# Scaling Wh by a bound from x and W, and carrying the bound as column 129, in a graph network's opening stage

## The chip, the cores and the metric

The kernel runs on one core of a Trainium2 chip. The metric is the device time of one execution in microseconds (us); lower is better.

## The reference

Two graph layers over 8192 nodes with 128 features, each followed by a residual and a layer norm. The adjacency matrix is 8192 x 8192 in int32 and has ones on its diagonal and about 0.1% of the other places.

```python
Wh = h @ W
a1, a2 = (a[:Fout, 0], a[Fout:, 0])
e = (Wh @ a1)[:, None] + (Wh @ a2)[None, :]
e = jnp.where(e > 0, e, ALPHA * e)                    # ALPHA = 0.2
e = jnp.where(adj > 0, e, MASK_VAL)
attention = jax.nn.softmax(e, axis=1)
return jax.nn.elu(attention @ Wh)                     # layer 0
...
x1 = a @ x / deg                                      # layer 1
return jnp.concatenate([x1, x], axis=1) @ weight + bias
...
x = _layernorm(x + layer0(x, adj, W, a), axis=-1)
x = _layernorm(x + layer1(x, adj, weight, bias), axis=-1)
```

With s = Wh a1 and t = Wh a2, exp of a positive score is exp(s) exp(t), and of a negative one exp(0.2 s) exp(0.2 t). So the softmax's sums are matrix products of two 0/1 masks (score positive, score negative, each within the edges) with two scaled copies of Wh.

## The kernel before

**The pieces.** The nodes are cut into 64 blocks of 128 (j). Sixteen steps k of four blocks make Wh; 32 groups g of 256 rows make layer 0, each in eight eighths h of eight blocks; two eighths make a unit c. Five engines run their own lists in order and wait for each other by semaphores.

**x and Wh.** SyncE loads x in nine pieces. In step k TensorE transposes four tiles of x (`turn_x`), ScalarE copies them out and at the same time sums them over the nodes (`copy_turned`, L416), and TensorE multiplies them with W and its two products with a (`make_wh`, L617). VectorE copies s and t out of the result (L865), ScalarE copies Wh (`copy_wh`), and VectorE finds the largest absolute value of that piece (L871). W is transposed first of all, and W a (L597) made from it, before x is touched.

**The adjacency.** GpSimd issues transfers of chunks of 512 rows by 2048 columns, cast to bytes. TensorE packs a chunk to bits (`pack_bits`, L640), ScalarE copies the words (`copy_words`). VectorE unpacks them to edges (L936).

**The factors.** With t's maximum over all partitions (from GpSimd) ScalarE makes the columns exp(t - max) and exp(0.2 (t - max)). VectorE multiplies 16 blocks of Wh with one of them (`make_product`, L923: product n is unit n // 2, part n % 2), ScalarE scales and rounds to 16 bits (`high_of`, L504), and VectorE writes what is left as a second 16-bit half (`low_of`, L1028; `low_half`, L1037). The scale comes from the largest absolute value of Wh, which goes through GpSimd once more. Column 129 of each half holds the exponential itself, for the denominators; VectorE makes these columns by casts and subtractions of their own. x lies in the space of the second part of the factors until it is no longer needed.

**The masks.** ScalarE compares t of a block with s of 256 rows (a score, `first_scores` L436 for group 0, `scores` L466 later). VectorE ands the eight scores of an eighth with the edges (`negative`, L1013) and then xors the edges with that (`positive`, L1020). TensorE multiplies both masks with the factors (`multiply`, L679), 32 matmuls an eighth; within the first group an eighth also waits for the low halves of its unit. Later chunks are packed between the multiplications of a group.

**Order in the opening.** ScalarE turns s around for the store of s (L452), makes scores 0 to 9, words 0, high halves 0 and 1, words 1, scores 10 to 29, the columns for u and v, high halves 2 and 3, scores to 49, words 2, high halves 4 and 5, the other scores, words 3, eight scores of group 1, and high halves 6 and 7. VectorE makes for each unit both low halves, the four masks, and the next two products. The sum over x's nodes, needed for rows without edges, is a reduction of ScalarE's sums.

Of the kernel before, what the change touches and what calls it, by code (L numbers as in the profile page):

```python
# [50 lines left out]
WIDEST = 10.0  # L51
# [7 lines left out]
def adj_resnorm_kernel(nc, x, adj, w0, a0, w1, b1, consts, out):  # L59
# [21 lines left out]
    with ctx:  # L81
# [3 lines left out]
        def sem(name):  # L85
# [11 lines left out]
        cols = sb("cols", [P, 12, NJ], F32)  # L97
# [9 lines left out]
        wh_top = sb("wh_top", [P, NX], F32)  # L107
        x_sums = sb("x_sums", [P, NX], F32)
# [5 lines left out]
        s_col, t_col, t_big, e_col, f_col, u_col, v_col, y_col, uy_col, vy_col, e_den, f_den = \  # L114
            (cols[:, k, :] for k in range(12))
        t_max, _, wh_max, wh_one, neg_t, neg_ft, inv_wh, scale_e, ones, sum_x = (one[:, k:k + 1] for k in range(10))
# [10 lines left out]
        wh = words[:, NG // 2:, :].rearrange("p g w -> p (g w)").bitcast(F32)[:, 0:NJ * F]\  # L127
            .rearrange("p (j f) -> p j f", f=F)
        early = words[:, 2:NG // 2, :].rearrange("p g w -> p (g w)").bitcast(F32)
        sizes, at, early_of = dict(product=3 * UNIT * F, wq=F + 2, w_turn=P, a_sb=2,  # L130
# [4 lines left out]
        product = early_of["product"].rearrange("p (k j f) -> p k j f", k=3, f=F)  # L135
        x_in = factors[:, 1, :, :].rearrange("p j r -> p (j r)").bitcast(F32)[:, 0:NJ * F]\
            .rearrange("p (k j f) -> p k j f", k=NX, f=F)
        x_t = product[:, 2, 0:2 * XB, :].rearrange("p (k j) f -> p k (j f)", k=2)
# [213 lines left out]
        def _(pool):  # L352
# [49 lines left out]
        def _(act):  # L402
# [3 lines left out]
            act.wait_ge(w0_turned, 1)  # L406
            act.activation(w_turn, turn_ps[0][:, 0:P], ACT.Copy).then_inc(w_turn_ok, 1)
            act.wait_ge(wa_made, 1)
            act.activation(wq[:, F:F + 2], turn_ps[1][:, 0:2], ACT.Copy).then_inc(wa_ok, 1)
# [15 lines left out]
            def copy_wh(k):  # L425

                act.wait_ge(wh_ok, k + 1)
                act.activation(wh[:, XB * k:XB * (k + 1), :].rearrange("p (h j) f -> p h j f", h=2),
                               wh_banks(k)[:, :, :, 0:F], ACT.Copy).then_inc(wh_copied, 1)
# [23 lines left out]
            first_scores(0, 2)  # L453


# [3 lines left out]
            first_scores(2, 10)  # L459
# [40 lines left out]
            def high_of(n):  # L500
# [3 lines left out]
                act.activation(factors[:, n % 2, (n // 2) * UNIT:(n // 2 + 1) * UNIT, 0:F], product[:, n % 3, :, :],  # L504
                               ACT.Copy, scale=scale_e).then_inc(high_ok, 1)
# [83 lines left out]
        def _(pe):  # L589
# [3 lines left out]
            pe.wait_ge(w0_in, 16)  # L593
            pe.transpose(turn_ps[0][:, 0:P], wq[:, 0:F], ident).then_inc(w0_turned, 1)
            pe.wait_ge(w_turn_ok, 1)
            pe.wait_ge(a0_in, 16)
            pe.matmul(turn_ps[1][:, 0:2], w_turn, a_sb, start=True, stop=True).then_inc(wa_made, 1)  # L597
            pe.wait_ge(wa_ok, 1)
            pe.wait_ge(ones_ok, 1)

# [10 lines left out]
            def make_wh(k):  # L611

                pe.wait_ge(x_t_ok, k + 1)
                if k >= 2:
                    pe.wait_ge(wh_copied, k - 1)
# [28 lines left out]
            def spread_s():  # L644

                pe.wait_ge(wh_ok, 1)
                for j in range(2 * TPG):
                    m = pe.matmul(pack_ps[1][:, j * P:(j + 1) * P], s_col[:, j:j + 1].to_broadcast([P, P]), ident,
                                  start=True, stop=True)
                m.then_inc(s_spread, 1)  # L650

            turn_x(0)
            for k in range(NX):
                if k + 1 < NX:
                    turn_x(k + 1)
# [42 lines left out]
            pe.wait_ge(wh_copied, NX)  # L698
            pack_bits(1)
            wide = is_wide(pe)  # L700
            pe.wait_ge(sum_xb_ok, 1)
            pe.matmul(turn_ps[1][:, 0:F], sum_xb, wq[:, 0:F], start=True, stop=True).then_inc(mean_made, 1)
            pe.wait_ge(den_hi_ok, 4)
            pe.wait_ge(edge_col_ok, 1)
            for c in range(UPG):
                for h in (2 * c, 2 * c + 1):
                    multiply(0, h, c == UPG - 1 or h % 2 == 0, True)
                if c < 2:
                    pack_bits(c + 2)
            group(1, {1: (1, 0), 2: (1, 1), 3: (1, 2)})  # L710
# [134 lines left out]
        def _(dve):  # L845
# [16 lines left out]
            def copy_s_t(k):  # L862

                dve.wait_ge(wh_made, k + 1)
                dve.tensor_copy(cols[:, 0:2, XB * k:XB * (k + 1)].rearrange("p k (h j) -> p h j k", h=2),  # L865
                                wh_banks(k)[:, :, :, F:F + 2]).then_inc(wh_ok, 1)

            def largest_wh(k):

                dve.wait_ge(wh_copied, k + 1)  # L870
                dve.tensor_reduce(wh_top[:, k:k + 1], wh[:, XB * k:XB * (k + 1), :], AX.XY,  # L871
                                  ALU.max, apply_absolute_value=True).then_inc(top_ok, 1)

            def scaled_t(c):

                dve.wait_ge(wh_ok, XB * (c + 1))
# [478 lines left out]
```

## Time and profile before

| | |
|---|---|
| time, median of 3 runs | 1486.75 us (1486.2 to 1486.85) |
| span of the profiled execution | 1484.3 us |
| what lies around the span, against the median | 2.45 us |
| TensorE busy | 1449.9 us (98%) |
| VectorE busy | 994.9 us (67%) |
| ScalarE busy | 936.4 us (63%) |
| GpSimd busy | 118.3 us (8%) |
| mean granted TensorE clock | 0.991 |

The span is from the first to the last instruction of the profiled execution; its own time beyond the span isn't recorded, so the median stands for it. Busy shares are averages over stages with different limits; a line such as L679 is a line of the kernel. PE is TensorE's matmul, PEld its weight load, DVE VectorE, ACT ScalarE, POOL GpSimd. The granted clock is 1.00 at 2.4 GHz and 0.50 at 1.2 GHz.

### The profile page before, as it was taken

The page shows a single profiled execution, that of the slowest core. Times are in us where ns is not written, and L with a number is a line of the kernel's source. Part 1 is how long each engine was busy: PE and PEld are TensorE (multiplying, and loading weights), DVE is VectorE, ACT ScalarE, POOL GpSimd, SP SyncE. Part 2 cuts the span into 40 slices and gives each one's busy share as a digit, 9 for nine tenths or more (in the row PEclk, how much of TensorE's full clock was granted, in tenths as well). Part 3 has the DMA queues.
Part 4 walks back from the last instruction along what each step waited for, and adds up shares of the span by engine and source line. Part 5 has one row for each costly group of instructions (what it writes and reads, how often), then busy time and mean ns, then how long its engine had stood idle before and what let it go on. Part 6 is the DMA issues. An engine that isn't in the chain of part 4 may idle for free.

```text
span 1484.3 us, 33988 instructions
## 1 busy us (share of the span) xinstructions
PE 1449.9 (98%) x12110; PEld 1107.8 (75%) x12110; DVE 994.9 (67%) x2833; ACT 936.4 (63%) x2289; POOL 118.3 (8%) x199
## 2 busy tenths in 40 slices
PE   7599999999999999999999999999999999999998
PEld 7578888888888888888888888884454545454557
DVE  4998888888788888878887887773433343334332
ACT  6989999999999999999999999940000000000000
POOL 1001000100010010001000100000000000000000
PEclk9799999999999999999999999999999999999999
DMA  9969997788788868877886882041000000000000
GB/s 174 111 71 101 120 108 90 83 94 95 84 86 96 93 78 95 94 90 82 95 94 83 87 96 37 19 119 49 22 15 21 14 21 14 21 14 21 14 15 15
DMA packets 99201, 101.47 MB, mean 68 GB/s; under 512 B 4432, under 2 KB 66384, under 8 KB 99152
## 3 DMA queue, kind: packets, MB, share of 16 engines
q0 software_dynamic: 33792, 67.11, 45.5%
q1 hardware_dynamic: 64800, 33.57, 8.7%
q8 instruction: 31, 0.51, 0.1%
q10 hardware_dynamic: 560, 0.14, 0.1%
q14 instruction: 18, 0.15, 0.0%
HBM read 289.48 MB, written 12.65 MB: 204 GB/s over the span
## 4 chain that ended last, share of the span: by engine, by line
PE 90%; DMA 2%; DVE 1%; issue 0%; POOL 0%; ACT 0%; SPq 0%; DVEq 0%; POOLq 0%
PE acc L679 58%; PE pack_ps L758 27%; PE pack_ps L819 2%; DMA adj_space<-in_adj 2%; PE acc L793 1%; PE pack_ps L628 1%; PE turn_ps L780 1%; PE turn_ps L769 0%; DMA level_ring<-x_rows 0%; DMA x_parts<-parts 0%; POOL one L378 0%; DVE adj_space L945 0%; DVE stats L1118 0%; DVE part_sums L1051 0%; DVE edge_ring L1020 0%
## 5 line engine op out<-in xcount | busy, mean ns | idle before, releaser
L466 ACT ACTIVATE level_ring<-s_row,cols 128x256 fp8e4<-128x256 f32 x1984 | 803.7, 495 | 0.0
L679 PE MATMUL acc<-factors,edge_ring 128*128 128x259 f16 x4096 | 548.8, 274 | 14.5 <-DVE edge_ring L1020 13.0
L679 PE MATMUL acc<-factors,level_ring 128*128 128x259 f16 x4096 | 548.3, 274 | 0.0
L758 PE MATMUL pack_ps<-adj_space,factors 128*128 128x512 fp8e4 x1920 | 421.7, 379 | 0.9 <-issue 0.9
L679 PEld LDWEIGHTS acc<-factors,edge_ring 128*128 128x128 fp8e4 x4096 | 365.9, 98 | 64.8 <-issue 15.8
L679 PEld LDWEIGHTS acc<-factors,level_ring 128*128 128x128 fp8e4 x4096 | 366.5, 98 | 48.9
L758 PEld LDWEIGHTS pack_ps<-adj_space,factors 128*128 128x128 f16 x1920 | 187.9, 98 | 217.6 <-issue 1.1
L1013 DVE TENSOR_TENSOR level_ring<-level_ring,edge_ring 128x1024 uint16<-128x1024 uint16 x256 | 171.2, 689 | 103.7 <-ACT level_ring L466 93.3
L1190 DVE TENSOR_SCALAR adj_space<-words 128x512 uint16 (+1 forms) x448 | 96.3, 288 | 146.7 <-PE pack_ps L758 146.6
L628 PE MATMUL pack_ps<-pack_w,adj_space 128*128 128x32 bf16 x960 | 170.7, 178 | 0.0
L1020 DVE TENSOR_TENSOR edge_ring<-edge_ring,level_ring 128x1024 uint16<-128x1024 uint16 x256 | 166.7, 683 | 0.1
L558 ACT ACTIVATE level_ring<-turn_ps 128x512 f32<-128x512 f32 x16 | 9.6, 597 | 217.4 <-PE turn_ps L769 217.4
L566 ACT ACTIVATE level_ring<-pack_ps 128x256 f32<-128x256 f32 x30 | 9.9, 381 | 212.6 <-PE pack_ps L758 212.6
L936 DVE TENSOR_SCALAR edge_ring<-words 128x512 uint16 (+1 forms) x448 | 106.1, 297 | 8.6 <-issue 6.4
L376 POOL TENSOR_SCALAR one<-mv 128x2 f32<-128x2 f32 x64 | 18.9, 295 | 1075.1 <-DVE mv L1125 1075.1
L628 PEld LDWEIGHTS pack_ps<-pack_w,adj_space 128*128 128x128 fp8e4 x960 | 91.6, 95 | 14.1
L1219 DVE SCALAR_TENSOR_TENSOR level_ring<-acc,cols,level_ring 128x128 f32<-128x128 f32 x64 | 19.4, 346 | 96.8 <-PE acc L793 96.8
L945 DVE SCALAR_TENSOR_TENSOR adj_space<-adj_space 128x1024 int32<-128x1024 int32 x60 | 73.1, 1218 | 0.9 <-DMA adj_space<-in_adj 0.9
L358 POOL DMA_DIRECT2D adj_space<-in_adj x64 | 51.3, 802 | 260.5 <-PE pack_ps L628 195.8
L422 ACT ACTIVATE words<-pack_ps 128x512 f32 (+1 forms) x64 | 38.1, 595 | 39.7 <-PE pack_ps L628 39.7
L378 POOL TENSOR_TENSOR one<-one 128x2 f32<-128x2 f32 x64 | 48.0, 750 | 9.5
L1130 DVE TENSOR_SCALAR level_ring<-level_ring,mv,one 128x128 f32<-128x128 f32 x64 | 19.3, 344 | 41.5 <-POOL one L378 41.5
(104 smaller groups left out, 726.8 us busy)
## 6 DMA issues: line engine op xcount, KB each, us to landing
adj_space<-in_adj POOLq DMA_DIRECT2D x64, 1024.0 KB, 14.5
rows_x<-in_x SPq DMA_DIRECT2D x32, 128.0 KB, 2.1
x_rows<-rows_y SPq DMA_DIRECT2D x32, 128.0 KB, 9.7
x_parts<-parts SPq DMA_DIRECT2D x32, 128.0 KB, 4.4
factors<-x_parts SPq DMA_DIRECT2D x8, 512.0 KB, 4.8
level_ring<-x_rows SPq DMA_DIRECT2D x16, 256.0 KB, 2.8
out<-level_ring SPq DMA_DIRECT2D x32, 128.0 KB, 1.8
s_row<-s_and_t SPq DMA_DIRECT2D x30, 128.0 KB, 3.0
```

The lines of the kernel that those rows point to most:

```text
L358: pool.dma_start(adj_ring[:, c, :, :], adj_tiles[n, :, :, c * COLS:(c + 1) * COLS]).then_inc(adj_in[c], 16)
L378: pool.tensor_tensor(rstd, var_eps, minus_half, ALU.pow).then_inc(rstd_sem, TPG)
L422: act.activation(row_words[:, n, c * WPU:(c + 1) * WPU], pack_ps[c % 2][:, 0:WPU], ACT.Copy)\
L466: a = act.activation(level_bytes[:, h % MASK_SLOTS, j, :], s_row[:, slot, :], ACT.Relu, bias=t_big[:, h * HALF + j:h * HALF + j + 1], scal ...
L628: return pe.matmul(pack_ps[c % 2][:, j * WPR:(j + 1) * WPR], nibbles, pack_w[:, 0, :], start=True, stop=True)
L679: m = pe.matmul(acc[a][:, 0:WIDE_ROW], mask, factors[:, neg, jj, 0:WIDE_ROW], start=(jj == 0), stop=(jj == NJ - 1))
L758: m = pe.matmul(pack_ps[slot][:, :], factors[:, 0, jj, part * F:(part + 1) * F], ring_1_bytes[:, c, j, :], start=(jj == 0 and part == 0), ...
L936: d = dve.tensor_scalar(to, src, 6 - k, EDGES, ALU.logical_shift_left, ALU.bitwise_and)
L945: dve.scalar_tensor_tensor(out=pair[:, 0], in0=pair[:, 1], scalar=1, in1=pair[:, 0], op0=ALU.logical_shift_left, op1=ALU.bitwise_or).then_ ...
L1013: dve.tensor_tensor(level, level, edge_ring[:, c % EDGE_SLOTS, k * HALF:(k + 1) * HALF, :], ALU.bitwise_and).then_inc(neg_ready, 1)
L1020: dve.tensor_tensor(edges, edges, level_ring[:, (2 * c + k) % MASK_SLOTS, :, :], ALU.bitwise_xor)\
L1190: d = dve.tensor_scalar(to, src, 6 - k, EDGES, ALU.logical_shift_left, ALU.bitwise_and)
```

## The change

All of it lies in the opening, up to the end of group 0.

- The scale of the factors no longer comes from the largest value of Wh, but from a bound: the largest absolute value of x, found on VectorE as x's pieces land (`top_of_x`), times the largest sum of absolute values over W. GpSimd makes both maxima in one call, before Wh is complete.
- Wh, s and t lie together, 130 columns a block. Even steps are copied by ScalarE (`copy_wh`), odd ones by VectorE (`keep_wh`), all 130 columns at once. Once s has been copied to its own columns, its place in each block gets the bound. VectorE's products are then 129 columns wide, and so are the high and low halves: the denominators' columns come with them, and their casts and subtractions go.
- The sum of x over the nodes is made by TensorE with a column of ones (`sum_rows_of_x`), behind the first pack, ahead of the transposition of s. x's space is needed until then, so high half 1 and a memset wait for it. VectorE copies and spreads the sum (`sum_of_x`).
- The columns y, uy and vy are made by GpSimd.
- W is transposed after x's first tile.
- The orders of ScalarE and VectorE in group 0 are written anew.
- The limit of t's spread from which another, slower path is taken goes from 10 to 7.5.

```diff
-WIDEST = 10.0
+WIDEST = 7.5
...
-        cols = sb("cols", [P, 12, NJ], F32)
+        cols = sb("cols", [P, 10, NJ], F32)
...
+        early = words[:, 2:, :].rearrange("p g w -> p (g w)").bitcast(F32)
+        sizes, at, early_of = dict(wh=NJ * (F + 2), product=3 * UNIT * FD, wq=F + 2, w_turn=P, a_sb=2,
...
+        wh_s_t = early_of["wh"].rearrange("p (j f) -> p j f", f=F + 2)
+        wh, wh_top = wh_s_t[:, :, 0:F], wh_s_t[:, :, 0:FD]
+        s_of, t_of = wh_s_t[:, :, F], wh_s_t[:, :, F + 1]
...
@@ gpsimd
+            pool.wait_ge(x_top_ok, NX // 2 + 2)
+            pool.wait_ge(w_sums_ok, 1)
+            pool.partition_all_reduce(tops[:, 2:4], tops[:, 0:2], P, bass.bass_isa.ReduceOp.max).then_inc(x_w_ok, 1)
             pool.wait_ge(t_top_ok, 1)
             pool.wait_ge(low_ok, 2)
             pool.partition_all_reduce(top_low[:, 2:4], top_low[:, 0:2], P, bass.bass_isa.ReduceOp.max).then_inc(t_max_ok, 1)
-            pool.wait_ge(wh_one_ok, 1)
-            pool.partition_all_reduce(wh_max, wh_one, P, bass.bass_isa.ReduceOp.max).then_inc(wh_max_ok, 1)
+            pool.wait_ge(t_max_ok, 1)
+            pool.wait_ge(cols_ok, 1)
+            pool.tensor_tensor(y_col, s_col, t_max.to_broadcast([P, NJ]), ALU.add).then_inc(y_ok_col, 1)
...
@@ scalar
-                act.activation(x_t[:, k % 2, :], turn_ps[k % 2][:, :], ACT.Copy, accum_out=x_sums[:, k:k + 1])\
-                    .then_inc(x_t_ok, 1)
+                act.activation(x_t[:, k % 2, :], turn_ps[k % 2][:, :], ACT.Copy).then_inc(x_t_ok, 1)
...
-            for k in range(NX):
+            copy_turned(0)
+            act.wait_ge(w0_turned, 1)
+            act.activation(w_turn, pack_ps[0][:, 0:P], ACT.Copy).then_inc(w_turn_ok, 1)
+            copy_turned(1)
+            act.wait_ge(wa_made, 1)
+            act.activation(wq[:, F:F + 2], pack_ps[0][:, P:P + 2], ACT.Copy).then_inc(wa_ok, 1)
+            copy_wh(0)
+            for k in range(2, NX):
                 copy_turned(k)
...
-                if k:
+                if k % 2:
                     copy_wh(k - 1)
-            copy_wh(NX - 1)
-            act.wait_ge(s_row_ok, 1)
-            act.wait_ge(s_turned, 1)
-            act.activation(s_turn, turn_ps[0][:, 0:P], ACT.Copy).then_inc(s_turn_ok, 1)
-            first_scores(0, 2)
+                if k >= 6:
+                    first_scores(k - 6, k - 5)
+            first_scores(10, 12)
+            copy_words(0, 0)
+            act.wait_ge(cols_ok, 1)
             act.wait_ge(neg_ok, 2)
             act.activation(e_col, t_col, ACT.Exp, bias=neg_t).then_inc(exp_cols_ok, 1)
             act.activation(f_col, t_col, ACT.Exp, bias=neg_ft, scale=ALPHA).then_inc(exp_cols_ok, 1)
-            first_scores(2, 10)
+            first_scores(12, 16)
+            act.wait_ge(s_turned, 1)
+            act.activation(s_turn, turn_ps[0][:, 0:P], ACT.Copy).then_inc(s_turn_ok, 1)
...
-            copy_words(0, 0)
             high_of(0)
+            first_scores(16, 20)
+            act.wait_ge(sum_made, 1)
             high_of(1)
+            first_scores(20, 24)
             copy_words(0, 1)
-            first_scores(10, 30)
+            first_scores(24, 32)
+            high_of(2)
+            high_of(3)
+            first_scores(32, 40)
+            copy_words(0, 2)
+            high_of(4)
+            high_of(5)
+            first_scores(40, 56)
+            high_of(6)
+            copy_words(0, 3)
+            first_scores(56, 64)
+            high_of(7)
             act.wait_ge(uy_ok, 2)
...
-            high_of(2)
-            high_of(3)
-            first_scores(30, 50)
-            copy_words(0, 2)
-            high_of(4)
-            high_of(5)
-            first_scores(50, 64)
-            copy_words(0, 3)
             scores(1, 1, 0)
-            high_of(6)
-            high_of(7)
...
@@ tensor
+            def sum_rows_of_x():
+
+                pe.wait_ge(ones_ok, 1)
+                for k in range(NX):
+                    for j in range(XB):
+                        m = pe.matmul(turn_ps[1][:, 0:1], x_in[:, k, j, :], ones, start=(k + j == 0),
+                                      stop=(k == NX - 1 and j == XB - 1))
+                m.then_inc(sum_made, 1)
...
-            pe.wait_ge(wh_ok, NX)
-            pe.transpose(turn_ps[0][:, 0:P], cols[:, 0:2, :].rearrange("p k j -> p (k j)"), ident).then_inc(s_turned, 1)
             pe.wait_ge(pack_w_ok, 2 * TILES - 1)
             pack_bits(0)
+            sum_rows_of_x()
+            pe.wait_ge(cols_ok, 1)
+            pe.transpose(turn_ps[0][:, 0:P], cols[:, 0:2, :].rearrange("p k j -> p (k j)"), ident).then_inc(s_turned, 1)
...
                     if factors_in and a < 2:
+                        pe.wait_ge(edge_col_ok, neg + 1)
                         pe.wait_ge((e_low_ok, f_low_ok)[neg], min(h // 2, UPG - 1) + h // 7 + 1)
...
@@ vector
+            def top_of_x(k):
+
+                dve.wait_ge(x_in_sem[k], 16)
+                first, end = max(2 * k - 1, 0), min(2 * k + 1, NX)
+                dve.tensor_reduce(x_top[:, k:k + 1], x_in[:, first:end], AX.XYZ, ALU.max, apply_absolute_value=True)\
+                    .then_inc(x_top_ok, 1)
+
+            def keep_wh(k):
 
                 dve.wait_ge(wh_made, k + 1)
-                dve.tensor_copy(cols[:, 0:2, XB * k:XB * (k + 1)].rearrange("p k (h j) -> p h j k", h=2),
-                                wh_banks(k)[:, :, :, F:F + 2]).then_inc(wh_ok, 1)
-
-            def largest_wh(k):
...
+                dve.tensor_copy(wh_s_t[:, XB * k:XB * (k + 1), :].rearrange("p (h j) f -> p h j f", h=2), wh_banks(k))\
+                    .then_inc(wh_kept, 1)
...
+            dve.tensor_scalar(wh_one, x_most, w_most, 1e-30, ALU.mult, ALU.max).then_inc(wh_one_ok, 1)
...
-            make_product(0)
-            scale_of_wh()
-            make_product(1)
-            for col, den in ((e_col, e_den), (f_col, f_den)):
-                dve.tensor_scalar(den, col, E_SCALE, None, ALU.mult).then_inc(den_ok, 1)
...
-            for c in range(UPG - 1):
-                low_of(2 * c, e_low_ok)
-                low_of(2 * c + 1, f_low_ok)
-                masks(0, 0, c)
-                make_product(2 * c + 2)
-                make_product(2 * c + 3)
-            last_masks_of_first()
...
+            def sum_of_x():
+
+                dve.wait_ge(sum_made, 1)
+                dve.tensor_copy(sum_x, turn_ps[1][:, 0:1]).then_inc(sum_x_ok, 1)
+                dve.wait_ge(sum_x_ok, 1)
+                dve.tensor_scalar(sum_xb, ident, 0.0, sum_x, ALU.mult, ALU.add).then_inc(sum_xb_ok, 1)
+
+            first_unpack(0)
+            make_product(0)
+            split(0, 0)
+            make_product(1)
+            low_of(0, e_low_ok)
+            split(0, 1)
+            dve.wait_ge(sum_made, 1)
+            dve.memset(factors[:, 1, :, ROW:WIDE_ROW], 1.0).then_inc(edge_col_ok, 1)
+            low_of(1, f_low_ok)
+            make_product(2)
+            first_unpack(1)
+            make_product(3)
+            split(1, 0)
+            split(1, 1)
+            low_of(2, e_low_ok)
+            low_of(3, f_low_ok)
+            make_product(4)
+            make_product(5)
+            first_unpack(2)
+            split(2, 0)
+            split(2, 1)
+            low_of(4, e_low_ok)
+            low_of(5, f_low_ok)
+            make_product(6)
+            make_product(7)
+            sum_of_x()
...
+            for k in range(2):
+                low_half(2 * UPG - 2, k, e_low_ok)
+                if k == 0:
+                    unpack(0, 0, UPG - 1, edge_ring, UPG - 1).then_inc(unpacked, 1)
+                low_half(2 * UPG - 1, k, f_low_ok)
+                negative(0, UPG - 1, k)
+                positive(0, UPG - 1, k)
```

## Rows read from the trace of the kernel before

**Rows 1.** Busy time by stretch; columns: engines' busy us (instructions), TensorE clock, DMA share, GB/s.
```profile
0.00:93.20 93.20, 67.38 (x718) 59.45 (x719) 70.71 (x130) 79.42 (x169) 7.38 (x15) 0.87 1.06 137
93.20:920.00 826.80, 825.91 (x8168) 728.43 (x8169) 677.10 (x1735) 775.28 (x1921) 77.08 (x112) 1.00 0.79 89
```

**Rows 2.** Waits of TensorE, first 200 us: us in total, times, longest.
```profile
PE acc L679 <- DVE edge_ring L1020: 13.0, 4, 7.3
```

**Rows 3.** Timeline of the opening: start, us, engine, line, operation, idle before.
```profile
7.14 0.56 PE L597 MATMUL turn_ps<-words 128*128 128x2 f32 x2 [1.62 <-DMA words<-in_a]
...
9.85 2.10 PE L617 MATMUL acc<-words 128*128 128x130 f32 x8
...
12.55 1.06 PE L617 MATMUL acc<-words 128*128 128x130 f32 x8
...
30.76 2.36 PE L617 MATMUL acc<-words 128*128 128x130 f32 x16
...
33.55 1.75 PE L640 MATMUL pack_ps<-pack_w,adj_space 128*128 128x32 bf16 x64
...
35.64 2.29 DVE L923 TENSOR_TENSOR words<-words,cols 128x2048 f32<-128x2048 f32 x1
...
39.35 3.89 ACT L504 ACTIVATE factors<-words,one 128x2048 f16<-128x2048 f32 x2
...
42.05 0.50 PEld L702 LDWEIGHTS turn_ps<-words 128*128 128x128 f32 x2 [1.06 <-DVE words L965]
...
50.12 1.89 PE L679 MATMUL acc<-factors,edge_ring 128*128 128x259 f16 x8 [7.28 <-DVE edge_ring L1020]
...
80.48 1.29 DVE L1037 SCALAR_TENSOR_TENSOR factors<-words,one,factors 128x1024 f16<-128x1024 f32 x1 [0.60 <-ACT factors L504]
...
88.12 0.69 DVE L1020 TENSOR_TENSOR edge_ring<-edge_ring,level_ring 128x1024 uint16<-128x1024 uint16 x1
...
93.21 1.05 PE L679 MATMUL acc<-factors,edge_ring 128*128 128x259 f16 x8 [0.54 <-DVE part_sums L1051]
```

**Rows 4.** Groups by form, first 93 us: busy us, mean ns, idle before.
```profile
L436 ACT ACTIVATE level_ring<-s_row,cols 128x256 fp8e4<-128x256 f32 x64 | 26.0, 497 | 0.0
...
L923 DVE TENSOR_TENSOR words<-words,cols 128x2048 f32<-128x2048 f32 x8 | 18.0, 2285 | 0.1
...
L504 ACT ACTIVATE factors<-words,one 128x2048 f16<-128x2048 f32 x8 | 15.7, 1995 | 0.9 <-DVE words L923 0.9
...
L1028 DVE SCALAR_TENSOR_TENSOR factors<-words,one,factors 128x2048 f16<-128x2048 f32 x6 | 14.0, 2373 | 0.2 <-ACT factors L504 0.2
...
L640 PE MATMUL pack_ps<-pack_w,adj_space 128*128 128x32 bf16 x256 | 7.1, 179 | 3.9 <-issue 3.9
...
L1013 DVE TENSOR_TENSOR level_ring<-level_ring,edge_ring 128x1024 uint16<-128x1024 uint16 x10 | 6.5, 687 | 0.1
...
L1037 DVE SCALAR_TENSOR_TENSOR factors<-words,one,factors 128x1024 f16<-128x1024 f32 x4 | 5.1, 1284 | 0.6 <-ACT factors L504 0.6
...
L936 DVE TENSOR_SCALAR edge_ring<-words 128x512 uint16<-128x512 uint16 x19 | 4.5, 297 | 0.1
...
L422 ACT ACTIVATE words<-pack_ps 128x512 uint16<-128x512 f32 x4 | 2.3, 578 | 0.0
...
L597 PE MATMUL turn_ps<-words 128*128 128x2 f32 x2 | 0.6, 348 | 1.6 <-DMA words<-in_a 1.6
```

**Rows 5.** Busy time and granted clock around the falls and rises.
```profile
33.50:36.40 2.90, 1.80 (x65) 1.69 (x65) 2.77 (x12) 2.63 (x8) 1.26 (x3) 1.00 1.05 107
36.40:50.10 13.70, 2.67 (x66) 2.30 (x67) 13.44 (x27) 13.70 (x28) 1.17 (x2) 0.50 1.06 116
50.10:53.20 3.10, 3.08 (x15) 2.16 (x16) 3.10 (x3) 2.38 (x7) 0.00 (x0) 0.50 1.07 107
71.20:74.00 2.80, 0.00 (x0) 0.00 (x0) 2.77 (x7) 2.80 (x8) 0.74 (x1) 0.99 1.06 108
74.00:80.10 6.10, 5.08 (x24) 3.57 (x25) 5.88 (x5) 6.10 (x12) 0.00 (x0) 0.50 1.05 116
```

More of the change, by code:

```diff
@@ L113, in adj_resnorm_kernel @@
         ident = consts_sb[:, 0:P]
-        s_col, t_col, t_big, e_col, f_col, u_col, v_col, y_col, uy_col, vy_col, e_den, f_den = \
-            (cols[:, k, :] for k in range(12))
-        t_max, _, wh_max, wh_one, neg_t, neg_ft, inv_wh, scale_e, ones, sum_x = (one[:, k:k + 1] for k in range(10))
+        s_col, t_col, t_big, e_col, f_col, u_col, v_col, y_col, uy_col, vy_col = \
+            (cols[:, k, :] for k in range(10))
+        x_most, w_most, _, wh_one, neg_t, neg_ft, inv_wh, scale_e, ones, sum_x = (one[:, k:k + 1] for k in range(10))
+        x_most, w_most = tops[:, 2:3], tops[:, 3:4]
         t_max, t_spread = top_low[:, 2:3], wide_one[:, 7:8]
@@ L592, in _ @@
             pe.wait_ge(consts_in, 16)
[L593 to L599, printed above, removed]
             def turn_x(k):
@@ L709, in _ @@
                     pack_bits(c + 2)
+                if c == 2:
+                    pe.wait_ge(sum_xb_ok, 1)
+                    pe.matmul(turn_ps[1][:, 0:F], sum_xb, wq[:, 0:F], start=True, stop=True).then_inc(mean_made, 1)
             group(1, {1: (1, 0), 2: (1, 1), 3: (1, 2)})
@@ L880, in _ @@
-            for k in range(NX):
-                copy_s_t(k)
-                if 0 < k < NX - 1:
-                    largest_wh(k - 1)
-                if k % XB == XB - 1 and k < NX - 1:
-                    scaled_t(k // XB)
-            dve.wait_ge(wh_ok, NX)
-            dve.tensor_reduce(top_low[:, 1:2], t_col, AX.X, ALU.min).then_inc(low_ok, 1)
-            dve.tensor_reduce(top_low[:, 0:1], t_col, AX.X, ALU.max).then_inc(t_top_ok, 1)
+                dve.tensor_scalar(t_big[:, js], t_of[:, js], -BIG, None, ALU.mult).then_inc(t_big_ok, 1)
@@ new lines, in _ @@
+            top_of_x(0)
+            dve.wait_ge(w_turn_ok, 1)
+            dve.tensor_reduce(tops[:, 1:2], w_turn, AX.X, ALU.add, apply_absolute_value=True).then_inc(w_sums_ok, 1)
+            top_of_x(1)
+            top_of_x(2)
+            keep_wh(1)
+            top_of_x(3)
+            top_of_x(4)
+            keep_wh(3)
+            scaled_t(0)
+            top_of_x(5)
+            keep_wh(5)
+            top_of_x(6)
+            keep_wh(7)
+            scaled_t(1)
+            top_of_x(7)
@@ new lines, in _ @@
+            top_of_x(8)
+            dve.wait_ge(x_top_ok, NX // 2 + 1)
+            dve.tensor_reduce(tops[:, 0:1], x_top[:, :], AX.X, ALU.max).then_inc(x_top_ok, 1)
+            keep_wh(9)
+            keep_wh(11)
+            scaled_t(2)
+            dve.wait_ge(x_w_ok, 1)
+            dve.tensor_scalar(wh_one, x_most, w_most, 1e-30, ALU.mult, ALU.max).then_inc(wh_one_ok, 1)
+            dve.wait_ge(wh_one_ok, 1)
+            dve.reciprocal(inv_wh, wh_one).then_inc(inv_ok, 1)
+            dve.wait_ge(inv_ok, 1)
@@ L902, in _ @@
             dve.tensor_scalar(wide_flag[:, :], t_spread, WIDEST, None, ALU.is_gt).then_inc(wide_ok, 1)
-            def scale_of_wh():
-                dve.wait_ge(wh_max_ok, 1)
-                dve.tensor_scalar(wh_one, wh_max, 1e-30, None, ALU.max).then_inc(guard_ok, 1)
-                dve.wait_ge(guard_ok, 1)
-                dve.reciprocal(inv_wh, wh_one).then_inc(inv_ok, 1)
-                dve.wait_ge(inv_ok, 1)
-                dve.tensor_scalar(scale_e, inv_wh, E_SCALE, None, ALU.mult).then_inc(scale_ok, 1)
+            dve.memset(factors[:, 0, :, ROW:WIDE_ROW], 1.0).then_inc(edge_col_ok, 1)
             def make_product(n):
@@ L1027, in low_of @@
                 dve.wait_ge(high_ok, n + 1)
-                dve.scalar_tensor_tensor(out=factors[:, k, js, FD:FD + F], in0=product[:, n % 3, :, :], scalar=scale_e,
-                                         in1=factors[:, k, js, 0:F], op0=ALU.mult, op1=ALU.subtract)\
+                dve.scalar_tensor_tensor(out=factors[:, k, js, FD:ROW], in0=product_of[n], scalar=scale_e,
+                                         in1=factors[:, k, js, 0:FD], op0=ALU.mult, op1=ALU.subtract)\
                     .then_inc(done, 1)
@@ L1036, in low_half @@
                 dve.wait_ge(high_ok, n + 1)
-                dve.scalar_tensor_tensor(out=factors[:, part, js, FD:FD + F],
-                                         in0=product[:, n % 3, k * HALF:(k + 1) * HALF, :], scalar=scale_e,
-                                         in1=factors[:, part, js, 0:F], op0=ALU.mult, op1=ALU.subtract).then_inc(done, 1)
+                dve.scalar_tensor_tensor(out=factors[:, part, js, FD:ROW],
+                                         in0=product_of[n][:, k * HALF:(k + 1) * HALF, :], scalar=scale_e,
+                                         in1=factors[:, part, js, 0:FD], op0=ALU.mult, op1=ALU.subtract).then_inc(done, 1)
             def add_negative(g, first=False):
```

122 lines of the change are left out of this document (53 added, 69 removed).

## Prediction

> **What bounds the kernel now.** I read the busy time of the engines by stretch first. In the first 93.2 us TensorE is busy for 67.38 us; from 93.2 to 920 us it is busy for all but a microsecond [rows 1]. So whatever the change does to the moment at which group 1's first multiplication starts (93.21 us) is carried to the end one for one: no later stage has idle time of TensorE in which a delay could vanish or to which a gain could be lost. The change touches nothing behind that moment.
>
> The waits of TensorE say who sets it: its longest, 13.0 us in four pieces, are for the masks that VectorE writes (L1020) [rows 2]. In the timeline the 16 products of x and W end at 33.1 us, VectorE's first product starts at 35.64, ScalarE's first high half at 39.35, group 0's first multiplication at 50.12, VectorE's last mask of group 0 starts at 88.12 and is done at 88.8; TensorE then has one eighth of the group left and starts group 1 at 93.21 [rows 3]. Between 36.4 and 80 us VectorE is busy in nearly all of the stretches shown that have work for TensorE or wait for it (13.44 of 13.70, 3.10 of 3.10, 5.88 of 6.10) [rows 5]. So the opening is VectorE's list of work: 8 products, 8 low halves, 4 unpacks, 8 mask pairs. I call its end E; before, E = 88.8.
>
> **What the change does to VectorE's list.** Prices by form [rows 4]: a product 2.285 (2.25 in a row, 18.0 over 8), a low half of 16 blocks 2.37 (2.31 in a row), a half of it 1.28, an unpack of four 0.9 (19 took 4.5), a mask pair (and, then xor, 0.69 each with a little overlap) 1.33, and on ScalarE a high half 1.96 (15.7 over 8), a copy of words 0.58, one score 0.405 (26.0 over 64). The 129th column makes a product 2064 elements instead of 2048, under 1% of 2.285, 0.02 each, 0.3 over all sixteen. Gone from the list are the denominators' casts and subtractions, y, uy, vy and the scale chain, some 2.5 us between the first product and the first low half; new are the copy and spreading of the sum, 0.65, and a memset, 0.17. The nine reductions of x, the copies of odd blocks and the scale found from the bound run while TensorE works through x (16 steps of 12 matmuls, 0.11 us apart: 1.06 less the last one's 0.287, over 7; 1.33 us a step). A step pair asks of VectorE about 1.2 + 0.65 and of ScalarE about 2.3 of 2.66 us (estimates from the spacing of their copies and scores), so TensorE stays the slower, and the stage's cost stays hidden; it would show if they passed 2.66. W's transposition moves behind x's first tile, which lets Wh begin about 1 us earlier. The end of x's stage then is about 32.1 instead of 33.1, and the first chunk is packed by 33.9 (1.75 us) [rows 3]. The maximum of t still has to go round through GpSimd, and an unpack now stands ahead of the first product, so that ends at about 38.5, against 37.9 before.
>
> List without waits: 4 unpacks 3.6, 8 products 18.2, 6 low halves 13.9, 4 halves of one 5.1, 8 mask pairs 10.6, the new 0.8: 52.2 us from 35.2, hence E = 87.4. That is the most that the list itself can give, 1.4 us. Three waits stand in it.
>
> **The sum of x on TensorE.** Before, x's sum fell out of ScalarE's copies. Now TensorE makes it, by 64 products of an f32 tile of x with one column, and it comes right behind the first pack. An f32 product that is no transposition is two instructions in this trace (L597: 128x2, x2), so 128 weight loads. The spacing of one: L597's two starts are 0.21 us apart (0.56 less 0.348), in a stretch in which L617's matmuls too ran at half of their later speed (2.10 for eight at 9.85, 1.06 at 12.55); the two loads of L702, at granted clock 0.50, take 0.50 us together, which fits a spacing near 0.2 and a last load that outlasts it [rows 3 to 5]. At full clock the nearest f32 rows are L617's, 0.11 apart with 130 columns: the upper bound. The lower bound is the pack's fp8 loads, 0.025 apart (1.75 less 0.18, over 63). I take the f32 rows with few columns, 0.20 at half clock and 0.105 at full.
>
> The Trainium skill ("TensorE: Matmul & The Clock Gate", sections "LDWEIGHTS (loading the stationary operand)" and "Weight-path perf modes — Fast Weight Load (FWL) and DoubleRow") has 107 ns for a load of 128 columns and the fast load for all but FP32; by it the sum would take 13.7 us at full clock, against 3.2 by the fp8 rows, and it speaks against the low end.
>
> Which clock? The nearest rows: the clock stood at 1.00 while the pack ran and at 0.50 one microsecond behind its end, at 36.4; the next pack and the two products behind it (2.67 us busy) ran at 0.50 and did not bring it back; the first multiplications of group 0 still had 0.50 for 3.1 us before it rose [rows 5]. After an idle stretch from 71.2 it fell at 74.0, 2.9 us in. I take it that the sum, one column each, lets it fall to 1.2 GHz some 2 us in: 20 loads at 0.105 and 108 at 0.20, S = 2.1 + 21.6 = 23.7 us. Full clock throughout: 128 x 0.105 = 13.4.
>
> What is queued behind it: on TensorE the transposition of s (0.5 us at half clock), then the pack of chunk 1; on ScalarE, whose order has the wait for that transposition *ahead of the first high half*, everything; on VectorE the low halves. High half 0 starts at T = 33.9 + S + 0.5 + 0.3 (the copy of s), so 58.4 with S = 23.7, against 39.35 before. VectorE has by then done two products, an unpack and one mask pair (42.0) and stands idle until T + 1.96. The chunk-1 pack, held to 39.2 by its transfer before, now ends near T + 1.5; ScalarE copies its words at T + 7.1, before VectorE asks for them at T + 10.4, so that costs nothing more.
>
> **Two waits in the new order.** (a) VectorE's mask pair (2,1) needs the scores up to 47. ScalarE makes them behind high half 5, which waits for product 5: 1.96 + 8 x 0.405 = 5.2 us after that product, where VectorE is ready after an unpack and one pair, 2.2. Idle: 3.0. (b) Low half 7 needs high half 7, which ScalarE makes after high half 6, a copy of words and 8 scores: 1.96 + 0.58 + 3.24 + 1.96 = 7.7 after product 6, while VectorE gets there after product 7, the sum's copy, a half and an unpack: 2.25 + 0.65 + 1.28 + 0.9 = 5.1. Idle: 2.6. Before, the same places lost 0.6 together [rows 3], since the scores to 49 were made before high half 4, and high half 7 followed 6 directly.
>
> **The sum.** From T on VectorE has 1.96 (waiting), 2.35, 1.33, 0.17, 2.35, 2.27, 0.9, 2.27, 2.66, 4.62, 4.49, 0.9, 2.66, 4.62, 4.49, 0.65, 1.28, 0.9, 1.28, 1.33, 2.5, 1.33 = 47.3, and 5.6 of the two waits: E = T + 52.9 = 111.3, 22.5 later than before. At the end TensorE has waited over 6 us for mask pair 6 (from the end of eighth 5 at T + 43 to T + 49), so that it starts eighth 6 at 0.50, as it did at 75 us after a shorter gap; that took 5 to 6 us where full clock takes 3.6 [rows 5], and about 1 us of it is left when group 1 begins. Together +23.5. The profiled execution's span is 1484.3 and the median 1486.75, so 2.45 us lie around the span and stay: **1510**, own range 1503 to 1515 (clock falling 1 to 3 us in, loads of 0.18 to 0.21).
>
> **Rivals.** *The clock holds* (S = 13.4): TensorE has no gap in the sum, and so far only gaps stood ahead of each fall. T = 48.1, E = 101.0, +12.2, and the 1 us: 1500 (1497 to 1503). For it: the clock fell only behind the pack's end. Against: narrow work at 36 to 50 us did not raise it. The skill's page on TensorE, section "HAM oscillation — how this bites in real kernels", puts the loss down to idle gaps alone; by that rule the clock would hold here, and the time would be this rival's.
>
> *The sum is cheap*, with loads as fast as the fp8 ones or nearly: up to S = 5.3 ScalarE has high half 0 ready when VectorE wants it at 42.0, and only the waits (a) and (b) are left: E = 87.4 + 5.6 = 93.0, +4.2, +1: 1492 (1490 to 1495). Against it: no f32 load in the trace is closer than 0.1 us.
>
> *Faster*: Wh's early start is worth more than I put it. Before, the first step of Wh starts at 9.85 and the second at 12.55, two steps' time at half speed; if TensorE is at full speed by then, and a0's landing at 7.1 is all that holds it, x's stage ends up to 3 us earlier, and with the shorter list E would be 84.4, 1482. It decides only if the sum's end stays under 39 and ScalarE stays ahead at (a) and (b); each of these alone outweighs it. About as unlikely is no change, from parts of both.
>
> That the constant WIDEST goes from 10 to 7.5 changes nothing: t's spread, estimated from the reference's factors (0.06, 0.06, 128 features), is about 3.6.
>
> **Chances.** Clock falls 0.52, clock holds 0.28, cheap sum 0.10, no change 0.05, faster 0.05. A measurement here tells 0.2% (3 us) from no change, so slower 0.90. The range: 1494 to 1515 holds nearly all of the first two and a corner of the third, 0.8.
>
> **What would show it.** The sum's 128 instructions behind the first pack, their spacing and the granted clock; ScalarE idle before the copy of s and VectorE idle before the first low half until T + 2; idle of 3.0 before the mask pair (2,1) (for ScalarE's scores) and 2.6 before low half 7; VectorE's last mask of group 0 at 111; all distances after group 1's start as before. The prediction is wrong if f32 loads with one column come much faster than 0.1 us, if x's stage grows, or if any wait of TensorE behind 93 us shrinks.

## The result, and the profile after

The changed kernel takes 1510.0 us (median of 5 runs, 1509.23 to 1510.21), against 1486.75 us for the kernel before (median of 5, 1486.2 to 1488.15): a ratio of 1.0153, with a 95% interval of 1.014 to 1.0165. It is 23.25 us slower. The span of its profiled execution is 1507.3 us, 23.0 more than before.

Busy time by stretch of the kernel after, in the columns of [rows 1]. The first two lines are the rest from group 1's start, cut at the same distance as before; the others follow the sum of x.

```profile
117.65:944.45 826.80, 826.80 (x8179) 729.35 (x8177) 677.68 (x1735) 779.50 (x1930) 75.61 (x112) 1.00 0.79 89
944.45:1507.30 562.85, 555.60 (x3217) 318.98 (x3215) 245.88 (x967) 80.60 (x199) 33.82 (x72) 1.00 0.09 26
...
34.60:36.00 1.40, 1.40 (x19) 1.40 (x15) 1.25 (x10) 1.22 (x4) 0.35 (x1) 1.00 1.04 113
36.00:37.00 1.00, 1.00 (x11) 1.00 (x10) 1.00 (x5) 1.00 (x3) 0.00 (x0) 1.00 1.09 109
37.00:38.00 1.00, 1.00 (x10) 1.00 (x9) 1.00 (x1) 0.56 (x2) 0.00 (x0) 0.89 1.04 104
38.00:39.00 1.00, 1.00 (x7) 1.00 (x6) 1.00 (x2) 0.00 (x0) 0.00 (x0) 0.50 1.05 106
39.00:58.80 19.80, 19.80 (x95) 19.80 (x95) 3.33 (x3) 0.00 (x0) 2.05 (x4) 0.50 1.06 108
```

From 34.6 to 58.8 us TensorE is busy without a gap, and all the same the granted clock goes from 1.00 to 0.50 within the two microseconds from 37. Ahead of the fall the products start 0.11 us apart (the first at 34.59, the 29th at 37.71), behind it 0.213 (the 30th at 37.88, the 128th and last at 58.79). In the last stretch shown VectorE is busy for 3.33 of 19.80 us and ScalarE not at all: both wait.

The timeline of the opening of the kernel after, as in [rows 3].

```profile
8.83 2.10 PE L623 MATMUL acc<-words 128*128 128x130 f32 x8 [0.53 <-ACT words L449]
11.58 1.94 PE L623 MATMUL acc<-words 128*128 128x130 f32 x8
14.03 1.06 PE L623 MATMUL acc<-words 128*128 128x130 f32 x8
...
32.98 1.75 PE L646 MATMUL pack_ps<-pack_w,adj_space 128*128 128x32 bf16 x64
...
34.59 24.55 PE L663 MATMUL turn_ps<-one,factors 128*128 128x1 f32 x128
...
46.30 0.48 POOL L377 TENSOR_SCALAR cols<-cols 128x64 f32<-128x64 f32 x1
...
59.49 0.28 ACT L470 ACTIVATE words<-turn_ps 128x128 f32<-128x128 f32 x1 [21.93 <-PE turn_ps L685]
59.67 2.02 ACT L515 ACTIVATE factors<-words,one 128x2064 f16<-128x2064 f32 x1
61.73 2.37 DVE L1033 SCALAR_TENSOR_TENSOR factors<-words,one,factors 128x2064 f16<-128x2064 f32 x1 [19.36 <-ACT factors L515]
65.41 2.44 DVE L1033 SCALAR_TENSOR_TENSOR factors<-words,one,factors 128x2064 f16<-128x2064 f32 x1
...
90.09 0.69 DVE L1018 TENSOR_TENSOR level_ring<-level_ring,edge_ring 128x1024 uint16<-128x1024 uint16 x1 [3.09 <-ACT level_ring L439]
...
105.97 1.29 DVE L1042 SCALAR_TENSOR_TENSOR factors<-words,one,factors 128x1032 f16<-128x1032 f32 x1 [2.94 <-ACT factors L515]
...
108.89 1.39 PE L703 MATMUL acc<-factors,edge_ring 128*128 128x259 f16 x8 [4.64 <-DVE edge_ring L1025]
111.64 0.69 DVE L1025 TENSOR_TENSOR edge_ring<-edge_ring,level_ring 128x1024 uint16<-128x1024 uint16 x1
117.65 1.05 PE L703 MATMUL acc<-factors,edge_ring 128*128 128x259 f16 x8
...
174.18 1.23 DVE L984 SCALAR_TENSOR_TENSOR adj_space<-adj_space 128x1024 int32<-128x1024 int32 x1 [0.47 <-DMA adj_space<-in_adj]
```

Read the brackets in order. The 128 instructions of the sum take 24.55 us. ScalarE, whose copy of s stands behind them, waits 21.93 us for it, and so the first high half starts at 59.67 instead of 39.35. VectorE waits 19.36 us for that half, then 3.09 us ahead of the mask pair (2,1) for scores, and 2.94 us for high half 7. Its last mask ends at E = 111.64 + 0.69 = 112.33 us; before it was 88.12 + 0.69 = 88.81. So E is 23.5 us later, which is the size of the loss.

### The profile page after: what moved, and what is told of

Read it like the earlier page. It is cut to its first block, busy times and chain, and to the rows that moved or that the text cites. A ratio compares the mean times of both kernels' runs of the same rounds, so it can differ in the third digit from the quotient of the medians.

```text
span 1507.3 us, 34219 instructions
## 1 busy us (share of the span) xinstructions
PE 1476.8 (98%) x12238; PEld 1134.1 (75%) x12238; DVE 998.4 (66%) x2813; ACT 931.4 (62%) x2265; POOL 117.9 (8%) x202
## 4 chain that ended last, share of the span: by engine, by line
PE 95%; DVE 2%; ACT 1%; DMA 1%; issue 1%; POOL 0%; SPq 0%; DVEq 0%; POOLq 0%
PE acc L703 60%; PE pack_ps L780 27%; PE pack_ps L841 2%; PE turn_ps L663 2%; PE acc L623 1%; PE pack_ps L634 1%; PE acc L815 1%; PE turn_ps L802 1%; DVE words L962 1%; ACT level_ring L439 1%; PE turn_ps L614 1%; DVE factors L1033 1%; PE turn_ps L791 0%; ACT factors L515 0%; DMA factors<-in_x 0%
## 5 line engine op out<-in xcount | busy, mean ns | idle before, releaser
L1270 DVE SCALAR_TENSOR_TENSOR level_ring<-acc,cols,level_ring 128x128 f32<-128x128 f32 x64 | 19.4, 346 | 96.7 <-PE acc L815 96.7
```

## The experiments

Two theories stand against each other. By the first, three things add up: the sum's length, which is long because its one-column products run at the low clock, and the waits (a) and (b), which come from ScalarE's order alone. By the rival, the loss lies in what the change needs anyway, wider products, new waits or x's stage, and the sum is only where it shows. Each time stands beside the kernel before, run on the same chip.

**The sum with 128 columns.** The same 128 weight loads, but each multiplies 128 columns of ones instead of one.

```diff
-                        m = pe.matmul(turn_ps[1][:, 0:1], x_in[:, k, j, :], ones, ...
+                        m = pe.matmul(turn_ps[1][:, 0:P], x_in[:, k, j, :], ones.to_broadcast([P, P]), ...
```

> The sum's 128 matmuls stream 128 columns of ones instead of one; the loads are the same. If the fall of the clock sets their spacing (my theory), wide matmuls behind the pack keep full clock, the spacing goes to 0.11 us, the sum takes 14 us instead of 24.5 and the kernel 1499 to 1501 us. If a load of f32 weights is 0.2 us apart for another reason than the clock, the time stays at 1509 to 1511 or grows, with the sum at 24 us or more. If the sum isn't what delays the opening, no change either, but with a sum of 14 us.

Measured: 1498.63 us beside 1487.21, ratio 1.0076 [1.006, 1.0093]. Its timeline, and then its clock during the sum:

```profile
34.16 14.54 PE L663 MATMUL turn_ps<-one,factors 128*128 128x128 f32 x128
...
101.00 0.69 DVE L1025 TENSOR_TENSOR edge_ring<-edge_ring,level_ring 128x1024 uint16<-128x1024 uint16 x1
```

```profile
34.20:48.50 14.30, 14.30 (x133) 14.30 (x130) 7.56 (x16) 2.78 (x7) 2.10 (x5) 1.00 1.06 108
```

128 times the columns, and the sum is 10.0 us shorter. The clock stands at 1.00 throughout, and the spacing is (14.54 - 0.27)/127 = 0.112 us, the 0.11 of the f32 rows with 130 columns. One-column products have it too, ahead of the fall. E comes 10.6 us earlier, the span is 10.5 us shorter (1496.8), and the loss against the kernel before goes from 23.25 to 11.4 us. So 10 of the 24.55 us are the clock's; the other 14.5 are the 128 loads with their products at the high level.

**The sum back on ScalarE.** x's sum falls out of ScalarE's copies again, and no engine waits for a sum of TensorE any more; nothing else is undone.

```diff
-                act.activation(x_t[:, k % 2, :], turn_ps[k % 2][:, :], ACT.Copy).then_inc(x_t_ok, 1)
+                act.activation(x_t[:, k % 2, :], turn_ps[k % 2][:, :], ACT.Copy, accum_out=x_sums[:, k:k + 1])\
+                    .then_inc(x_t_ok, 1)
...
-            act.wait_ge(sum_made, 1)
...
-            sum_rows_of_x()
...
-                dve.wait_ge(sum_made, 1)
-                dve.tensor_copy(sum_x, turn_ps[1][:, 0:1]).then_inc(sum_x_ok, 1)
+                dve.wait_ge(x_t_ok, NX)
+                dve.tensor_reduce(sum_x, x_sums[:, :], AX.X, ALU.add).then_inc(sum_x_ok, 1)
```

> The sum over x's nodes goes back to ScalarE's copies, as in the kernel before; nothing waits for TensorE's sum any more, all else as changed. My theory: ScalarE starts high half 0 near 38.8 us, VectorE's list runs on from 42.4, its last mask is done near 93.3 instead of 112.3, and the time is 1490 to 1492. Rival, the 129 columns and the new list are what costs: over 1500. Rival, the copies with a sum slow x's stage by more than 1 us: 1493 or more.

Measured: 1491.06 us beside 1487.21, ratio 1.0026 [1.0016, 1.0036]: 19.4 of the 23.25 us are gone. Its timeline:

```profile
41.60 2.36 DVE L1033 SCALAR_TENSOR_TENSOR factors<-words,one,factors 128x2064 f16<-128x2064 f32 x1
...
70.07 0.69 DVE L1018 TENSOR_TENSOR level_ring<-level_ring,edge_ring 128x1024 uint16<-128x1024 uint16 x1 [3.09 <-ACT level_ring L441]
...
85.96 1.29 DVE L1042 SCALAR_TENSOR_TENSOR factors<-words,one,factors 128x1032 f16<-128x1032 f32 x1 [2.96 <-ACT factors L517]
...
91.62 0.69 DVE L1025 TENSOR_TENSOR edge_ring<-edge_ring,level_ring 128x1024 uint16<-128x1024 uint16 x1
```

The first low half is back at 41.60, without a wait. Both waits are still there, (a) with 3.09 us and (b) with 2.96: they belong to the order, not to the sum. E is 92.31. The copies with a sum do not slow x's stage: the pack starts at 32.30 here, at 32.98 in the kernel after.

**s turned ahead of the sum.** The transposition of s moves from behind the sum to ahead of it, so that ScalarE and high half 0 no longer wait.

```diff
             pack_bits(0)
-            sum_rows_of_x()
             pe.wait_ge(cols_ok, 1)
             pe.transpose(turn_ps[0][:, 0:P], cols[:, 0:2, :].rearrange("p k j -> p (k j)"), ident).then_inc(s_turned, 1)
+            sum_rows_of_x()
```

> The transposition of s stands ahead of the sum on TensorE, so that ScalarE's first high half no longer waits for the sum; high half 1 and VectorE's memset still do. My theory: VectorE goes on from low half 1 at 61.6 us instead of 65.4, so 3 to 4 us are won: 1506 to 1507. Rival, the wait ahead of high half 0 is the whole loss: 1490 to 1492.

Measured: 1506.55 us beside 1487.21, ratio 1.0129 [1.0112, 1.0145]. Its timeline:

```profile
35.36 24.93 PE L663 MATMUL turn_ps<-one,factors 128*128 128x1 f32 x128
...
60.33 2.04 ACT L515 ACTIVATE factors<-words,one 128x2064 f16<-128x2064 f32 x1 [17.40 <-PE turn_ps L663]
62.40 2.37 DVE L1033 SCALAR_TENSOR_TENSOR factors<-words,one,factors 128x2064 f16<-128x2064 f32 x1 [1.69 <-ACT factors L515]
...
108.56 0.69 DVE L1025 TENSOR_TENSOR edge_ring<-edge_ring,level_ring 128x1024 uint16<-128x1024 uint16 x1
```

Only 3 to 4 us come back (E by 3.1). The wait moves one place down: high half 1 writes where x lies, so it must wait for the sum in any order, 17.40 us here. The order of the two on TensorE is a small part; that x's space is held is the larger one.

**ScalarE's order.** The sum stays; the scores that a mask pair needs are made before the next high halves, and words 3 and the last scores before high half 6.

```diff
-            first_scores(32, 40)
+            first_scores(32, 48)
             copy_words(0, 2)
             high_of(4)
             high_of(5)
-            first_scores(40, 56)
-            high_of(6)
+            first_scores(48, 64)
             copy_words(0, 3)
-            first_scores(56, 64)
+            high_of(6)
             high_of(7)
```

> Only ScalarE's order in group 0 changes: scores 32 to 47 ahead of high half 4, scores 48 to 63 and words 3 ahead of high half 6, so that high half 7 follows 6 directly. My theory: the waits of 3.1 us (scores) and 2.9 us (high half 7) go, and 0.6 comes back: 1504 to 1505. Rival, they are hidden by TensorE's own work at the end of group 0: 1509 to 1510.

Measured: 1503.09 us beside 1487.21, ratio 1.0107 [1.009, 1.0124]: 7 us come back, a little more than the 6.03 us of both waits. Its timeline:

```profile
94.86 2.03 ACT L515 ACTIVATE factors<-words,one 128x2064 f16<-128x2064 f32 x1 [1.48 <-DVE words L961]
...
97.08 2.03 ACT L515 ACTIVATE factors<-words,one 128x2064 f16<-128x2064 f32 x1 [0.18 <-DVE words L961]
...
105.03 0.69 DVE L1024 TENSOR_TENSOR edge_ring<-edge_ring,level_ring 128x1024 uint16<-128x1024 uint16 x1
...
110.12 1.05 PE L702 MATMUL acc<-factors,edge_ring 128*128 128x259 f16 x8 [0.39 <-DVE part_sums L1055]
...
170.49 1.05 PE L702 MATMUL acc<-factors,edge_ring 128*128 128x259 f16 x8 [1.06 <-DVE part_sums L1055]
```

Now it is ScalarE that waits for VectorE's products at the last two high halves. E is 105.72, 6.6 us earlier, and group 1 starts 4.40 us after it, as before (4.40), instead of 5.32. The last line shown, a wait of TensorE in a later stage, is taken up with the prediction's last term below.

**Both.** The edits of the second and the fourth experiment together.

> Both repairs together: the sum on ScalarE's copies and ScalarE's order without the two waits. If the two losses add (my theory), VectorE's list runs without a wait of more than 0.6 us, its last mask is done near 86 to 88 us and the time is 1484 to 1486, so the rest of the change is worth 0 to 3 us. Rival, the 129 columns and VectorE's copies in x's stage cost as much as the denominators did: 1487 or more.

Measured: 1484.51 us beside 1487.37, ratio 0.998 [0.9971, 0.9989]: 2.9 us faster than the kernel before, and the fastest here. Its timeline:

```profile
8.52 2.10 PE L623 MATMUL acc<-words 128*128 128x130 f32 x8 [0.62 <-ACT words L451]
11.26 1.29 PE L623 MATMUL acc<-words 128*128 128x130 f32 x8
...
32.22 1.75 PE L646 MATMUL pack_ps<-pack_w,adj_space 128*128 128x32 bf16 x64
...
45.21 2.44 DVE L1032 SCALAR_TENSOR_TENSOR factors<-words,one,factors 128x2064 f16<-128x2064 f32 x1
45.46 2.49 POOL L378 TENSOR_SCALAR cols<-cols 128x64 f32<-128x64 f32 x1
...
85.22 0.69 DVE L1024 TENSOR_TENSOR edge_ring<-edge_ring,level_ring 128x1024 uint16<-128x1024 uint16 x1
90.31 1.05 PE L702 MATMUL acc<-factors,edge_ring 128*128 128x259 f16 x8 [0.39 <-DVE part_sums L1055]
```

E is 85.91, 2.9 us ahead of 88.81, and group 1 starts 2.9 us earlier. Alone the two edits gained 19.4 and 7.4 us, 26.8 in sum; together they gained 26.1 (23.25 + 2.86). So the sum and ScalarE's order make up all of the loss, and the rest of the change taken together (the bound, the 129th column with its wider products, VectorE's copies and order, the place of W) is a gain of 2.9 us.

**Three products on GpSimd.** On top of that, products 3, 5 and 7 are made by GpSimd, which is nearly idle, in the place of Wh. GpSimd then issues some of group 1's transfers of adjacency between them.

```diff
+            def pool_product(n):
...
+                pool.tensor_tensor(product_of[n], wh_top[:, js, :],
+                                   f_col[:, js].unsqueeze(2).to_broadcast([P, UNIT, FD]), ALU.mult)\
+                    .then_inc(pool_product_ok, 1)
...
-            make_product(3)
+            make_product(4)
...
-            make_product(4)
-            make_product(5)
+            make_product(6)
...
-            make_product(6)
-            make_product(7)
```

> As the run with both repairs, and GpSimd makes products 3, 5 and 7, in place in Wh, while VectorE goes on with masks. If VectorE's list is the bound of the opening, 3 x 2.27 = 6.8 us go from it, of which ScalarE's own list (scores, high halves, words: 39 us from 35.9 on) lets at most 5 through: 1480 to 1482. Rival, a product on GpSimd takes over 8 us or slows VectorE, so that the high halves wait for it: 1486 or more.

Measured: 1489.7 us beside 1487.37, ratio 1.0018 [1.0009, 1.0027], 5.2 us slower than without. Its timeline, POOL against DVE:

```profile
53.17 8.29 POOL L402 TENSOR_TENSOR words<-words,cols 128x2064 f32<-128x2064 f32 x2
...
53.84 4.12 DVE L1037 TENSOR_TENSOR level_ring<-level_ring,edge_ring 128x1024 uint16<-128x1024 uint16 x1
57.99 4.01 DVE L1044 TENSOR_TENSOR edge_ring<-edge_ring,level_ring 128x1024 uint16<-128x1024 uint16 x1
61.93 0.68 DVE L1037 TENSOR_TENSOR level_ring<-level_ring,edge_ring 128x1024 uint16<-128x1024 uint16 x1
...
70.20 4.21 POOL L402 TENSOR_TENSOR words<-words,cols 128x2064 f32<-128x2064 f32 x1 [7.99 <-DVE words L981]
70.95 4.01 DVE L1037 TENSOR_TENSOR level_ring<-level_ring,edge_ring 128x1024 uint16<-128x1024 uint16 x1
```

A GpSimd product takes some 4.2 us, and the VectorE mask that starts during it takes 4.0 to 4.1 us instead of 0.69; the first mask behind it takes 0.68 again. Three masks lose 10 us, and three products of 2.3 us save 7: 3 us of the loss. The other 2 us were not taken apart by a run. In this trace the pack starts 0.8 us later than in "both" (33.03), and group 1 starts 6.44 us after VectorE's last mask (96.69 against 90.25) instead of 4.40. The Trainium skill ("SBUF — State Buffer", section "Who interferes with whom") says that VectorE and GpSimd share a pair of ports as an exclusive lock, and that an instruction of VectorE with two inputs in SBUF is blocked fully while GpSimd reads; the three masks agree with it.

**W first again.** On top of "both", W is transposed ahead of x's first tile, as it was before the change.

```diff
-            turn_x(0)
             pe.wait_ge(w0_in, 16)
             pe.transpose(pack_ps[0][:, 0:P], wq[:, 0:F], ident).then_inc(w0_turned, 1)
-            turn_x(1)
...
             pe.wait_ge(wa_ok, 1)
+            turn_x(0)
+            turn_x(1)
```

> As the run with both repairs, but W is transposed before x's first tile, as in the kernel before. My forecast put the later transposition at 1 us won. If so, x's stage ends 1 us later and the time is 1 us above the run with both repairs. Rival, what ends x's stage is when TensorE's clock rises, and the order of W is lost in that: no difference beyond 0.5 us.

Measured: 1485.55 us beside 1487.37, ratio 0.9986 [0.9977, 0.9995], 1.04 us slower than with W later. Its timeline:

```profile
9.84 2.10 PE L623 MATMUL acc<-words 128*128 128x130 f32 x8
12.59 1.12 PE L623 MATMUL acc<-words 128*128 128x130 f32 x8
...
33.38 1.75 PE L646 MATMUL pack_ps<-pack_w,adj_space 128*128 128x32 bf16 x64
```

The first step of Wh starts 1.32 us later than in "both" and the pack 1.16 us later, so the place of W may be worth about 1 us. It isn't shown: the eleven times of each kernel overlap (1484.14 to 1486.53 against 1482.85 to 1485.13), and over the traces of the seven kernels with W later the pack starts anywhere between 32.22 and 33.43, so one trace can't tell. The expectation's rival, that the moment at which TensorE reaches its speed decides, stays open.

## Why the prediction was right, point by point

1510 was forecast and 1510.0 measured, by the mechanism that was forecast. Its terms were each a little off, and the errors cancelled: the mechanism held, as the experiments show, but that the number was met so closely is luck.

- **x's stage.** Forecast: the first chunk packed by 33.9; measured: the pack at 32.98 + 1.75 = 34.7, some 0.8 late. Wh did begin 1.02 us earlier (8.83 against [rows 3]'s 9.85), but its second step then took 1.94 us, where before it took 1.06 and in "both" 1.29: TensorE reached its speed later, and most of the microsecond was lost again. What sets that moment was not settled. The pack starts between 32.22 ("both") and 33.43 in the traces of the kernels with W later, and the 0.8 lies within that spread.
- **The sum.** Forecast 23.7 us, measured 24.55. The products start 0.11 and 0.213 us apart, against 0.105 and 0.20 taken, and the clock fell 3.2 us in, not 2. The rival in which the clock holds was refuted for one column; with 128 columns the clock holds, and the sum is 14.54 us long. The cheap sum was refuted as well: even at the high level the products are 0.11 us apart.
- **T.** Forecast 58.4, measured 59.67: 0.7 from the start of the sum, 0.85 from its length, less 0.3 in the two steps behind it.
- **The waits.** (a) forecast 3.0, measured 3.09. (b) forecast 2.6, measured 2.94. Both go with ScalarE's order alone.
- **VectorE's list.** E - T was forecast as 52.9 and measured as 52.66, with waits 0.4 longer; so the list is about 0.7 us shorter than its sum of prices. By itself it was to give 1.4 us; in "both", where no wait of VectorE is left in it, E is 2.9 us earlier than before. This term was sized at half of what it is worth, the place of W included.
- **The microsecond at the low clock.** TensorE waited 4.64 us ahead of eighth 6 (forecast: over 6) and ran it slowly, and group 1 started 5.32 us after E instead of 4.40: 0.92, as forecast. But it did not reach the end, and here a step of the prediction failed: "no later stage has idle time of TensorE in which a delay could vanish". A wait of TensorE behind 93 us did shrink, which the prediction had named as a sign of being wrong. These are rows of the kernel before, in its timeline and, behind that, its last stretch:

```profile
150.85 1.23 DVE L945 SCALAR_TENSOR_TENSOR adj_space<-adj_space 128x1024 int32<-128x1024 int32 x1 [0.90 <-DMA adj_space<-in_adj]
...
153.41 1.05 PE L679 MATMUL acc<-factors,edge_ring 128*128 128x259 f16 x8 [0.88 <-DVE part_sums L1051]
```

```profile
920.00:1484.30 564.30, 556.63 (x3227) 319.89 (x3224) 247.06 (x970) 81.69 (x202) 33.87 (x72) 1.00 0.09 26
```

VectorE waits there for a transfer of adjacency, and TensorE waits 0.88 us for VectorE: it is the missing microsecond of [rows 1], which the prediction saw and counted as nothing. That work of VectorE starts 62.0 us after E before the change and 61.9 after it (174.18 - 112.33), so it hangs on E and not on TensorE. A TensorE that is 0.92 us late against E no longer waits for it: its idle time from group 1's start on is 0 of 826.80 us after, against 0.89 before. The other kernels bear this out. Where group 1 starts 4.4 us after E (before, the fourth, fifth and seventh experiments), TensorE waits there, 0.67 to 1.06 us, as in the fourth's line at 170.49. Where it starts 5.3 us after E or later (after, the first, second, third and sixth), that wait is gone, and the span from group 1's start on is about a microsecond shorter: 1389.6 to 1389.9 us against 1390.6 to 1391.1. In the two stretches together 1.45 us come back (826.80 + 564.30 against 826.80 + 562.85): 0.89 here, 0.4 less idle in the last stretch, the rest within 0.2 us of busy time.

So the sum that holds is 23.5 (E) + 0.9 (the low clock) - 1.4 (given back later) = 23.0, the difference of the two spans; forecast were 22.5 + 1 + 0. E a microsecond too early and a late microsecond that did not last made up for each other. What lies between the profiled span and the median, 2.45 us in the prediction, came out as 2.7 (1510.0 - 1507.3).

## What to carry to other kernels

Before work is moved to an engine with time to spare, look at what stands behind it in that engine's order, and whose space it holds: before, the sum cost ScalarE 16 short reads of 0.2 us, one beside each copy of x, in a stage that TensorE set; on TensorE, busy for 67 of 93 us, it held up two engines for 20 us. Price it at both clocks, also when it has no gap. Where an order is written anew, follow for each wait the chain "what must the other engine do first": both waits of ScalarE's new order could be read from the prices beforehand to within 0.4 us, and the change without them and without TensorE's sum is a gain. A microsecond of idle time in a later stage is a place where a microsecond can vanish; see which engine sets that stage's start before you add a delay up to the end.

## What the runs showed of the hardware

- The granted clock fell from 1.00 to 0.50 (2.4 to 1.2 GHz) during uninterrupted work of TensorE, in f32 products with one column, and it did not with 128 columns and the same loads: 24.55 us against 14.54. In the two other kernels with the one-column sum (s turned first, ScalarE's order) it fell as well, 2.6 and 3.0 us in. The rule of the Trainium skill that the prediction weighed ("TensorE: Matmul & The Clock Gate", section "HAM oscillation — how this bites in real kernels"), which puts the fall down to idle gaps, doesn't cover this; the measurement decides.
- An f32 load with its product was spaced 0.213 us at the low level with one column, and 0.11 at the high one, with one column (34.59 to 37.71 us in the kernel after) as with 128. Here the number of columns changed the clock, and not the spacing at one level.
- GpSimd and VectorE hold each other up, in both directions. GpSimd's step over 128x64 elements took 0.48 us while VectorE stood idle (at 46.30 in the kernel after) and 2.49 us beside a low half of VectorE (at 45.46 in "both"); and VectorE's masks took 4.0 us beside a product of GpSimd.
